# Sigmoid rounded on ScalarE and the gate scaled on GpSimd, with four small edits in the stages before

## What is computed

```
def act_qdq(x):
    qmax = 2.0 ** (ACT_BITS - 1) - 1.0
    scale = jnp.maximum(jnp.max(jnp.abs(x)) / qmax, 1e-12)
    return jnp.clip(jnp.round(x / scale), -qmax - 1.0, qmax) * scale

def fixed_qdq_u16(x):
    scale = 1.0 / 65536.0
    return jnp.clip(jnp.round(x / scale), 0.0, 65535.0) * scale
x = act_qdq(x)
up = act_qdq(x @ lpbq_dequant(w_up).T)
gate = act_qdq(x @ lpbq_dequant(w_gate).T)
sig = fixed_qdq_u16(jax.nn.sigmoid(gate))
gate = act_qdq(gate * sig)
o = act_qdq(gate * up)
return o @ lpbq_dequant(w_down).T
```

## Time and profile before

| | us |
|---|---|
| median of 3 runs | 1693.31 |
| lowest and highest | 1690.7, 1693.75 |
| the profiled execution, its own time | 1693.09 |
| its span in the trace | 1691.3 |

### The profile page before, as it was taken

One profiled execution on the slowest core, in us unless ns is written; L12 is line 12 of the kernel. 1 busy time (PEld: TensorE's weight loads), 2 busy tenths in 40 slices (PEclk: granted clock), 3 DMA queues, 4 the chain that ended last, 5 costly groups with the idle time before them and its releaser, 6 DMA issues. The chain is left out here.

```text
span 1691.3 us, 30154 instructions
## 1 busy us (share of the span) xinstructions
PE 1451.7 (86%) x10725; PEld 1365.3 (81%) x10725; DVE 1200.4 (71%) x2590; ACT 959.1 (57%) x2100; POOL 846.9 (50%) x705
## 2 busy tenths in 40 slices
PE   5389999999999999995699999999998566889039
PEld 4269899999999989985699999999998555788039
DVE  7648788888888888784246666666577398459896
ACT  4547676767676767672444544544444344469542
POOL 4468576868686868572345555455544332000000
PEclk9679999999999999997799999999999778899569
DMA  7490202121212120001666566666655401003413
GB/s 250 146 323 32 75 20 82 32 82 32 82 32 82 32 73 14 26 14 35 244 206 206 184 213 183 186 202 191 212 156 171 103 29 40 7 28 110 141 33 110
DMA packets 91309, 186.94 MB, mean 111 GB/s; under 512 B 8568, under 2 KB 64184, under 8 KB 90904
## 3 DMA queue, kind: packets, MB, share of 16 engines
q1 hardware_dynamic: 80648, 171.19, 30.0%
q0 software_dynamic: 10512, 13.83, 4.7%
HBM read 139.01 MB, written 59.35 MB: 117 GB/s over the span
## 5 line engine op out<-in xcount | busy, mean ns | idle before, releaser
L1651 POOL TENSOR_TENSOR expert_w<-expert_raw,expert_w 128x768 fp32r<-128x768 f32 x95 | 181.9, 1916 | 242.0 <-ACT expert_w L1475 242.0
L1433 PE MATMUL psum<-slots_high,expert_w 128*128 128x384 f32 x1216 | 289.8, 339 | 6.3 <-DVE expert_act L1617 5.1
L884 ACT ACTIVATE expert_raw<-psum,neg_max 120x376 f32<-120x376 f32 (+2 forms) x384 | 176.9, 487 | 95.8 <-DVE neg_max L1087 92.9
L1433 PEld LDWEIGHTS psum<-slots_high,expert_w 128*128 128x128 f32 x1216 | 211.6, 190 | 9.9 <-issue 8.2
L1513 ACT ACTIVATE expert_act_high<-expert_act 128x384 fp32r<-128x384 f32 x152 | 79.8, 525 | 181.3 <-DVE expert_act L1617 181.3
L1110 DVE TENSOR_TENSOR pt_low<-psum,pt_high 128x752 fp32r<-128x752 f32 x128 | 120.5, 942 | 82.8 <-ACT pt_high L893 82.7
L1444 PE MATMUL psum<-expert_w,expert_act_high 128*128 128x256 f32 x912 | 173.3, 286 | 3.1 <-ACT slot_out L1495 2.9
L1622 DVE TENSOR_TENSOR expert_act_low<-expert_act,expert_act_high 128x384 fp32r<-128x384 f32 x152 | 109.8, 722 | 80.0 <-ACT expert_act_high L1513 80.0
L1006 POOL TENSOR_TENSOR qk_low<-rotated,qk_high 128x376 fp32r<-128x376 f32 x128 | 126.8, 991 | 66.8 <-ACT qk_high L877 66.5
L1433 PE MATMUL psum<-slots_low,expert_w 128*128 128x384 f32 x608 | 155.7, 337 | 0.0
L1444 PEld LDWEIGHTS psum<-expert_w,expert_act_high 128*128 128x128 f32 x912 | 145.4, 189 | 5.6 <-ACT slot_out L1495 3.9
(11 more groups left out here) (305 smaller groups left out, 3993.0 us busy)
## 6 DMA issues: line engine op xcount, KB each, us to landing
expert_w<-experts_split SPq DMA_DIRECT2D x57, 768.0 KB, 4.3
expert_raw<-in_experts SPq DMA_DIRECT2D x95, 384.0 KB, 5.7
x_slots<-in_c_slots SPq DMA_DIRECT2D x4, 3168.0 KB, 28.8
slot_rows<-x_slots SPq DMA_DIRECT2D x19, 396.0 KB, 5.5
up_spill<-held SPq DMA_DIRECT2D x5, 1128.0 KB, 5.0
held<-up_spill SPq DMA_DIRECT2D x5, 1128.0 KB, 5.8
whole_w<-in_experts SPq DMA_DIRECT2D x12, 384.0 KB, 4.5
experts_split<-pt_high SPq DMA_DIRECT2D x12, 384.0 KB
```

The lines of the kernel that those rows point to most:

```text
L884: last = act.activation(probs[0:ni, h % 2, at:at + P * it + ni], score_bank(h % 2, it), ACT.Exp, bias=neg_max[0:ni, h % 2, it:it + 1], acc ...
L1433: last = pe.matmul(psum[:, 2 * k + g % 2, 0:TILE_SLOTS], w[hw][:, f, at:at + P], xt[hx][:, i % 2, c, :], start=(n == c == 0), stop=(n == 2 ...
L1651: pool.tensor_tensor(w[1][:, g % RING, :], raw[:, r % RAW, :], w[0][:, g % RING, :].bitcast(F32), ALU.subtract).then_inc(w_low, 1)
```

## The change

In the last network, `scale_gate` goes from ACT to a new block of POOL, as one `tensor_scalar` with two operations, 16 instructions without a wait between them. ACT writes the sigmoid into two slots of f32 (`SIGS`), and a new `round_sig` on ACT multiplies it by 65536 and writes unsigned 16-bit integers, which round and saturate, into four slots of `sig_steps`. DVE's `ready_sig` is gone, and `up_peak` comes first in each unit. A sigmoid of one element (`sigmoid_warm`) is placed behind the last `keep` of the gate.

In the recurrence, a square root of one element (`sqrt_warm`) comes first on ACT, and `inverse2` is issued between the two instructions of `scan(i, 1)`. At the attention's start the two memsets of `v` count on a semaphore of their own, for which PE waits ahead of the first product with `v`. At the experts' start the second half of the first tile's rows goes to another bank, and SP waits for the rows of the first tile before it issues weights.

```
@@ attention
-        CLEARED = 6
+        CLEARED, V_CLEARED = 4, 2
                     pe.wait_ge(pt_ready, 16 * b + h + 1 + CR_PT)
+                    if b == h == 0:
+                        pe.wait_ge(v_cleared, V_CLEARED)
...
-                    pool.memset(v[part].rearrange("p t c (k n) -> p (t c) k n", k=3)[:, :, 1, :].bitcast(F32), 0.0).then_inc(cleared, 1)
+                    pool.memset(v[part].rearrange("p t c (k n) -> p (t c) k n", k=3)[:, :, 1, :].bitcast(F32), 0.0).then_inc(v_cleared, 1)
@@ expert_tiles
+        def turn_bank(i, c):
+
+            return BANK_TURN - 1 if i == 0 and c == 1 else BANK_TURN
...
                 rows_of(0)
+                sp.wait_ge(x_in[0], 16)
                 for i in range(N):
...
-                    if 2 * i + c:
+                    if i:
                         pe.wait_ge(x_low, 2 * i + c)
@@ recurrence
+                act.activation(warm[:], consts[:, EPS_LN:EPS_LN + 1], ACT.Sqrt)
                 act.wait_ge(prepared, 1)
...
                         last = dve.tensor_tensor_scan(state[:, u, k, c, :], decay[:, c:c + 1].broadcast_to((P, TOK)),
                                                       fed[:, u, k, c, :], lasts[k][:, c:c + 1], ALU.mult, ALU.add)
+                        if c == 0 and k == 1 and here(b - 2):
+                            inverse2(b - 2)
...
-                    if here(i - 2):
+                    if here(i - 2) and not here(i):
                         inverse2(i - 2)
@@ quantised_ffn
-                def scale_gate(m):
-                    c, t = half(m)
-                    act.activation(gate[:, c, t], gate[:, c, t], ACT.Identity, scale=I_GATE, bias=magic).then_inc(gate_scaled, 1)
-
                 def sigmoid(m):
                     c, t = half(m)
                     act.wait_ge(gate_scaled, m + 1)
+                    if m >= SIGS:
+                        act.wait_ge(sig_ready, m - SIGS + 1)
+                    act.activation(sig[:, m % SIGS, :, :], gate_low[:, c, t], ACT.Sigmoid, scale=S_GATE).then_inc(sig_made, 1)
+
+                def round_sig(m):
+                    act.wait_ge(sig_made, m + 1)
                     if m >= RING:
                         act.wait_ge(prod_made, m - RING + 1)
-                    act.activation(sig[:, m % RING, :, :], gate_low[:, c, t], ACT.Sigmoid, scale=S_GATE).then_inc(sig_made, 1)
+                    act.activation(sig_steps[:, m % RING, :, :], sig[:, m % SIGS, :, :], ACT.Copy,
+                                   scale=SIG_STEPS).then_inc(sig_ready, 1)
...
+                act.activation(warm[:], consts[:, EPS_LN:EPS_LN + 1], ACT.Sigmoid)
                 act.wait_ge(steps_made, STEP_GATE + 1)
-                scale_gate(0)
                 for m in range(UNITS):
-                    if m + 1 < UNITS:
-                        scale_gate(m + 1)
                     sigmoid(m)
                     keep(UNITS + m)
+                    round_sig(m)
...
-                def ready_sig(m):
-                    s = sig[:, m % RING, :, :]
-                    dve.wait_ge(sig_made, m + 1)
-                    dve.tensor_scalar(s, s, SIG_MAGIC, SIG_MAGIC + 1 - 1 / SIG_STEPS, ALU.add, ALU.min).then_inc(sig_ready, 1)
...
                 for m in range(UNITS):
-                    ready_sig(m)
+                    up_peak(m)
+                    weigh(m)
                     if m:
                         act_peak(m - 1)
-                    weigh(m)
-                    up_peak(m)
...
+            @block.gpsimd
+            def _(pool):
+                def scale_gate(m):
+                    c, t = half(m)
+                    pool.tensor_scalar(gate[:, c, t], gate[:, c, t], I_GATE, magic, ALU.mult, ALU.add).then_inc(gate_scaled, 1)
+
+                pool.wait_ge(steps_made, STEP_GATE + 1)
+                for m in range(UNITS):
+                    scale_gate(m)
```

17 lines of the change are left out of this document (10 added, 7 removed).

## The result

The changed kernel takes 1669.66 us (median of 4 runs, 1669.21 to 1669.86), against 1693.53 before (4 runs, 1690.7 to 1694.41). The ratio is 0.9862, with a 95% interval from 0.9844 to 0.9879: 1.4% faster. The forecast was 1671.0, from 1666.5 to 1682.0. The profiled execution took 1669.62 us, its span is 1667.8, so 23.5 us less span than before.

The account below looks back on a forecast made before the run. DVE was taken to bound the last network's loop and the recurrence's steady part. Gains 9.5 (loop) + 9.6 + 1.3 + 1.6 + 0.5 = 22.5 off the profiled 1693.09 gave 1670.6, adjusted and rounded to 1671.0 us, range 1666.5 to 1682.

Parts of the forecast that it names:

- `ready_sig`, 10.6 us: Last network's loop: 16 instructions leave DVE, its period per unit falls from 4.37 to 3.71, saving 10.6 us.
- The scaling's length p: Duration of one gate scaling on GpSimd, taken as 1.4 us, with 1.0 and 2.55 kept as ends.
- The holding, 2.6 us: In the loop `weigh` waits for GpSimd's scaling, p x ceil(2.48/p) - 2.48 per turn, 8 turns, costing 2.6 us.
- the prediction's gains there: Rival, longer scaling: loop gains 5.1 at p 1.7, 1.5 at 2.0, loses 4.8 at 2.4; total 1675 to 1685; chance 0.18.
- The loop's start: Last network: first maximum starts at 1510.6, not 1511.94, with the table load moved into the wait for the gate's step.
- Recurrence and table load: Recurrence: moving `inverse2` saves six waits of 1.6 us, 9.6; the table load moved into idle ACT time saves 1.3.
- The rival of half the gain: Recurrence: PE and ACT could be late once DVE stops waiting; 4.8 us less gain, total 1675.5; chance 0.10.
- Attention: Attention's start: PE, ACT and DVE wait for DVE's small memsets instead of the memset of `v_low`, saving 1.6 us.
- Experts: Experts' start: second turn no longer late, but SP's wait delays weights; +0.5 us taken, bounds -1.5 and +1.5.
- The scaling that never lets `weigh` in: Rival in the loop: first `weigh` waits for all 16 scalings; total 1679 to 1685 with short p, chance 0.07.
- The break-even it named: Rival, slower than before: `weigh` never let in with long p, deciding above p 1.9; total 1703.6 at 2.55; chance 0.04.
- Code loading: Rival: GpSimd loads code before the first scaling, some 6 us if only with the first instruction; total 1677; chance 0.03.

Follow-up runs that it names:

- the memset of 1128 elements: Changed kernel with a memset of the same size in place of each GpSimd scaling, so GpSimd only writes: 1668.71 us, one run.
- the addition of two tensors: Changed kernel with GpSimd's scaling made a long addition of two tensors, without multiplying by the inverse step: 1668.88 us, one run.
- `inverse2` alone: Kernel before with only `inverse2` moved between the two scan instructions, no square root of one element: 1682.02 us, ratio 0.9944.
- The square root alone: Kernel before with the three stage-start edits (attention's memsets, experts' bank and SP wait, square root of one element): 1690.86 us, ratio 0.9987.
- the thirds: Changed kernel with each GpSimd scaling split into three instructions of 376 elements: 1670.81 us, one run.

## Why the prediction was right

The forecast missed by 1.3 us, and the mechanisms it named for DVE are the ones that the runs show. That it came so close is in part luck: its terms were off by +1.5, +0.4, +0.55 and -0.1 us and three stretches that it left alone (before the attention, the gate, the rest) by -1.3, and the holding of `weigh` in this execution was 0.5 us where the same loop lost 2.8 and 3.5 in others.

1. *`ready_sig`, 10.6 us.* Right. The period fell from 4.37 to 3.72 (maxima of `up` at 1504.98 and 1508.71), and ACT, whose rounding took 1166 ns where 1150 to 1200 were worked out, stayed below it at 3.25. ACT idle between units, one of the signs that the prediction named, was not seen: it ran ahead without a pause.
2. *The scaling's length p.* 1.29 us by itself, where 1.4 was taken between 1.0 and 2.55. The ends were good: the memset of 1128 elements took 1.057 and the addition of two tensors 2.605. Taking half of the two-input slope was 0.1 too much. The best case of the Trainium skill ("GPSIMD Engine Reference", 3.1 Elementwise), some 1.8 cycles per element and so 1.69 us by estimate, is above what was measured. The same section has 1.03 cycles for an operation as short as this one, which is 0.97 us by estimate before any fixed part; the pieces of 376 and the whole of 1128 elements, 0.64 and 1.27 us from start to start, have a slope of 0.84 ns per element and agree with that.
3. *The holding, 2.6 us.* The mechanism was right and the size was a draw. With p = 1.27 from start to start the formula of the prediction gives 0.06 a turn, 0.5 in eight turns. The changed kernel's profile has 0.5, but in two turns (0.06 and 0.42) and nothing in the others, so the formula meets the sum and not the turns. And a `weigh` that comes as a scaling ends may as well wait for the next, and did, three times in one trace and twice in another. The term holds as 0.5 to 3.5. Between p = 1.3 and 2.6 it was not tried, and the prediction's gains there (5.1, 1.5 and -4.8) don't come out of it: with the eight turns of its own sum they are 4.5, -0.6 and -7.4.
4. *The loop's start.* The first maximum was to start 3.9 us after the step and did. The second came 0.55 late, behind ACT's copy, which wasn't in the sum. So the loop: 10.6 for `ready_sig`, 1.3 for the start, less 0.55 and 0.5, is 10.9 of the 11.0 measured, against 9.5.
5. *Recurrence and table load.* 11.3 against 9.6 + 1.3. The sum was right by two errors that cancel. `inverse2` alone gives 11.3: five waits nearly as priced (7.7), and the sixth more than double (3.6), since the tail is PE's and ACT's chain, not DVE's, and ran at the lower clock in part. The step of the prediction that failed is "what follows is PE's and ACT's chain" as mere cover: in the tail that chain was what `inverse2` released. The square root alone gives 0.1 to 0.4, not 1.3; behind `inverse2` it gave nothing in seven kernels and 1.5 in two. The rival of half the gain is refuted: DVE stayed 98% busy.
6. *Attention.* 1.6 at the start, exactly (PE starts 1.05 us after DVE's first memset, 2.64 before); the stage gave 2.15 in this pair of traces and 3.2 by the averages of ten and four. The rest goes with the shorter fall of the clock at its end, for which the prediction had no term.
7. *Experts.* 0.4 against 0.5, but this is not shown: the kernels without the two edits have 530.95 to 531.36, those with both 530.43 to 531.14. SP's wait does make the weights late, by 1.3 us at the first silu, and nothing of it is left at the end. That the rows land earlier, the reason for the +0.5, was not followed.
8. *The rivals.* The scaling that never lets `weigh` in was refuted in its full form, at p = 1.29 and at 2.6; a mild form is real, in the thirds, once for five pieces. The break-even it named was for a case that doesn't occur: with p = 2.6 the loop is 65.9 and still 8 us faster than before, since GpSimd and `weigh` take turns. Code loading didn't show: GpSimd's first instruction starts 0.1 us behind the step in each kernel.

The gate phase and what follows the loop came out 0.3 and 0.5 longer, neither touched by the change. Among the fourteen traces they vary by 0.9 and 1.2, so no cause is claimed.

## What to carry to other kernels

An instruction that is far too long for its shape and stands right behind the release of another engine's work may be waiting for that work: see whether both end together, place it ahead of the release, and look at what it releases in the stage's tail, where it can be worth more than its own wait. When work goes to GpSimd, count DVE's instructions with two SBUF inputs, and `tensor_scalar` in f32, not only the time that it frees; and if its length divides into the gap between them nearly evenly, pace it by a semaphore. One trace of such a loop is one draw: the same loop lost 0.5, 2.8 and 3.5 us. This loop got shorter by its longest column only, so a move off one engine and a move onto the other have to be judged together.

## What the runs showed of the hardware

- GpSimd's `tensor_scalar` with two operations on 128x1128 f32 took 1.29 us (128x376: 0.67), its `memset` 1.057, its addition of two tensors 2.605. The cost of the second input was 1.3 us.
- DVE's product with two inputs in SBUF and DVE's `tensor_scalar` in f32 wait for a GpSimd instruction that reads, and GpSimd's for theirs (2.48 us for 1.29). Maxima with one input, and GpSimd's memset, do neither.
- A waiting DVE instruction isn't always served at the next end of a GpSimd instruction: it was passed over by five short ones (4.72 us for 1.32).
- With an edit that starts a stage 1.6 us sooner went a shorter fall of the granted clock some 690 us later: some 7 us at the lower level in the four kernels with the old start, some 3.5 in the ten with the new one (by the shares of the three slices), and a stage shorter by 3.2 us on average. What ties them is not shown.
- In the tail of the recurrence, behind 3.44 us of idle PE, the granted clock was 0.50 and a pair of small products took 0.65 us; behind 1.94 us of it the clock was 1.00 and the pair took 0.39.
